# Attention by halves of the queries, in batches of four score units and four value units

## The reference

```
attn = einsum('bhnd,bhsd->bhns', q, k) * scale
attn = clip(attn, -11.0, 11.0)
attn = softmax(attn, axis=-1)
out  = einsum('bhns,bhsd->bhnd', attn, v)
x    = x + tanh(g_xattn) * (out @ Wo + bo)
```

## Time and profile before

| | |
|---|---|
| median of 3 runs (lowest to highest) | 1573.42 us (1571.2 to 1574.33) |
| profiled execution | 1573.17 us, span 1571.3 us |
| busy: TensorE / its weight loads | 1493.8 us (95%) / 868.4 us (55%) |
| busy: VectorE | 1323.4 us (84%) |
| busy: ScalarE | 701.4 us (45%) |
| busy: GpSimd | 132.6 us (8%) |
| mean granted TensorE clock | 0.992 |
| exps, 512 of them | 496.2 us |
| adds to prob_sum, 224 in the trace's group | 515.9 us |
| clips, 256 | 313.8 us |

### The profile page before, as it was taken

How to read it: one execution, slowest core, us unless ns; L and a number is a source line. 1 busy time by engine, 2 the same in 40 slices (tenths; PEclk the granted TensorE clock), 3 DMA queues, 4 the chain that set the end, 5 groups by cost and what they waited for, 6 DMA issues and landing times. The chain is left out here.

```text
span 1571.3 us, 22090 instructions
## 1 busy us (share of the span) xinstructions
PE 1493.8 (95%) x7888; PEld 868.4 (55%) x7896; DVE 1323.4 (84%) x1272; ACT 701.4 (45%) x778; POOL 132.6 (8%) x71
## 2 busy tenths in 40 slices
PE   3999999999998999999999999999999999998875
PEld 3788888888885344444444444444444444445553
DVE  7866667666746998999999999999999999997997
ACT  3442222222224555555555555555555555552221
POOL 2310000000001300000000000000000000005553
PEclk9999999999999999999999999999999999999998
DMA  5674565555587242253154044144234325105331
GB/s 191 243 255 169 172 190 161 189 158 168 165 241 221 80 122 69 68 135 98 50 121 121 27 121 121 45 103 121 66 82 126 77 65 135 41 28 134 128 113 53
DMA packets 121998, 195.30 MB, mean 124 GB/s; under 512 B 18368, under 2 KB 67520, under 8 KB 115808
## 3 DMA queue, kind: packets, MB, share of 16 engines
q1 hardware_dynamic: 119360, 190.49, 41.8%
q10 hardware_dynamic: 2592, 4.20, 0.7%
HBM read 114.70 MB, written 79.95 MB: 124 GB/s over the span
## 5 line engine op out<-in xcount | busy, mean ns | idle before, releaser
L932 ACT ACTIVATE prob<-score_ps 128x1024 f32<-128x1024 f32 x512 | 496.2, 1021 | 379.7 <-PE score_ps L861 379.5
L1016 DVE TENSOR_TENSOR prob_sum<-prob_sum,prob 128x2048 f32<-128x2048 f32 x224 | 515.9, 2303 | 0.5
L874 PE MATMUL value_ps<-prob,v_st 128*64 128x512 f32 x2048 | 497.4, 606 | 10.5 <-DVE prob L1022 10.1
L861 PE MATMUL score_ps<-q_st,k_st 64*128 64x512 f32 x3072 | 425.7, 409 | 2.5 <-PEq L102 2.1
L861 PEld LDWEIGHTS score_ps<-q_st,k_st 64*128 64x128 f32 x3072 | 268.7, 184 | 256.2 <-ACT prob L932 187.8
L1022 DVE TENSOR_SCALAR prob<-prob 128x2048 f32<-128x2048 f32 x256 | 313.8, 1226 | 68.1 <-ACT prob L932 64.2
L874 PEld LDWEIGHTS value_ps<-prob,v_st 128*64 128x64 f32 x2048 | 124.4, 136 | 250.5 <-issue 202.3
L645 DVE TENSOR_TENSOR k_cos<-k_raw,rope 128x1024 f32<-128x1024 f32 x32 | 39.2, 1225 | 99.9 <-ACT k_raw L546 99.9
L1305 POOL TENSOR_TENSOR o_lo<-o_in,o_hi 128x1024 fp32r<-128x1024 f32 x16 | 39.0, 2438 | 879.5 <-POOLq L115 872.6
L551 ACT ACTIVATE v_out<-proj_ps 128x1024 f32<-128x1024 f32 x31 | 32.0, 1031 | 136.6 <-PE proj_ps L228 136.6
L546 ACT ACTIVATE k_raw<-proj_ps 128x1024 f32<-128x1024 f32 x31 | 31.9, 1029 | 105.2 <-PE proj_ps L228 104.0
(11 more groups left out here) (118 smaller groups left out, 1294.1 us busy)
## 6 DMA issues: line engine op xcount, KB each, us to landing
k_st<-k_scr SPq DMA_DIRECT2D x128, 256.0 KB, 6.2
k_scr<-k_hi SPq DMA_DIRECT2D x64, 256.0 KB, 2.7
v_scr<-v_out SPq DMA_DIRECT2D x32, 512.0 KB, 3.5
k_scr<-k_lo SPq DMA_DIRECT2D x64, 256.0 KB, 3.9
q_st<-q_scr SPq DMA_DIRECT2D x16, 1024.0 KB, 10.3
v_st<-v_scr SPq DMA_DIRECT2D x16, 1024.0 KB, 13.2
q_scr<-q_hi SPq DMA_DIRECT2D x32, 256.0 KB, 3.6
q_scr<-q_lo SPq DMA_DIRECT2D x32, 256.0 KB, 3.7
```

Source lines behind the costliest of these rows:

```text
L861: last = pe.matmul(score_ps[:, half, a, :], k_st[slot][rows, k_part, s * P:(s + 1) * P], q_st[slot][rows, q_part, cols], start=(t == 0), s ...
L874: last = pe.matmul(value_ps[rows, cols], v_st[slot][:, s, rows], prob[:, s % PSLOT, a, cols], start=(s == 0), stop=(s == STEPS - 1))
L932: act.activation(prob[:, s % PSLOT, :, cols], score_ps[:, half, :, :], ACT.Exp, scale=SCALE).then_inc(exped, 1)
L1016: dve.tensor_tensor(total, total, prob[:, s % PSLOT, :, :], ALU.add).then_inc(added, 1)
```

## The change

Attention goes by halves of the queries. A unit is one key tile against 512 queries; a pair has 32 units, the first 16 for the first half. They are taken in 8 batches of four. TensorE does the scores of four units, then the values of the four units of the batch before. The scores have three slots of two banks, the values one bank, which is copied out after each half; the sums are taken for each half with 32 columns a matmul, in one bank, for both halves of `prob_sum`'s columns and both heads, and VectorE joins the two parts with a small add. The clip covers a whole batch (128 x 4096), the adds of the same batch follow it directly. `prob` holds two batches and has its former size. The chain of the reciprocals, the normalisation and the output store run once for each half of a pair, and the load two pairs ahead moves behind the first half's chain. All of `quantise_rhs` now stands in pair 0, three operations a batch.

```diff
-    PSLOT = 4
+    BATCH_UNITS = 4
+    UNITS = 2 * STEPS
+    BATCHES = UNITS // BATCH_UNITS
+    HALF_BATCHES = BATCHES // 2
+    BANKS = 3
+    ADDS = 2 * HALF_BATCHES - 1
-    prob = sb("prob", [P, PSLOT, 2, NQ])
-    prob_sum = sb("prob_sum", [P, 2, 2, NQ])
+    prob = sb("prob", [P, 2, BATCH_UNITS, 2 * CH])
+    prob_sum = sb("prob_sum", [P, 2, 2, 2, CH])
-    score_ps = ps("score_ps", [P, 2, 2, NQ // 2])
-    value_ps = ps("value_ps", [P, NQ])
-    sum_ps = ps("sum_ps", [P, NQ])
+    score_ps = ps("score_ps", [P, BANKS, 2, CH])
+    value_ps = ps("value_ps", [P, CH])
+    sum_ps = ps("sum_ps", [P, CH])
...
-    WO_STEPS = (3, 9, 11, 13)
+    WO_BATCHES = (1, 3, 4, 5)
...
+        def after(n, where, before, loading=None):
+            ends.store_sums(sp, n, 0)
+            ends.load_sums(sp, n, 0)
+            if before is not None:
+                ends.store_output(sp, n - 1, 1, *before)
+            ends.store_reciprocals(sp, n, 0)
+            ends.load_reciprocals(sp, n, 0)
+            if loading is not None:
+                load(n + 2, *loading)
+            ends.store_sums(sp, n, 1)
+            ends.load_sums(sp, n, 1)
+            ends.store_output(sp, n, 0, *where)
+            ends.store_reciprocals(sp, n, 1)
+            ends.load_reciprocals(sp, n, 1)
...
+        def scores(n, slot, b):
+            if b == 0:
                 pe.wait_ge(kqv_in[slot], KQV * (n // 2 + 1))
+            for u in range(b * BATCH_UNITS, (b + 1) * BATCH_UNITS):
+                half, s = divmod(u, STEPS)
+                cols = slice(half * CH, (half + 1) * CH)
+                if u >= BANKS:
+                    pe.wait_ge(exped, UNITS * n + u - BANKS + 1)
+                elif not first(n):
+                    pe.wait_ge(exped, UNITS * n - (UNITS - 1 - u) % BANKS)
...
+        def values(n, slot, b):
+            pe.wait_ge(clipped, BATCHES * n + b + 1)
+            if b % HALF_BATCHES == 0 and not (first(n) and b == 0):
+                pe.wait_ge(late.o_copied, 2 * n + b // HALF_BATCHES)
+            for i in range(BATCH_UNITS):
+                s = (b * BATCH_UNITS + i) % STEPS
                 for a in range(2):
                     rows = slice(a * DHEAD, (a + 1) * DHEAD)
+                    last = pe.matmul(value_ps[rows, :], v_st[slot][:, s, rows], prob[:, b % 2, i, a * CH:(a + 1) * CH],
                                      start=(s == 0), stop=(s == STEPS - 1))
...
+        def sums(n, half):
...
+            for j in range(2):
                 for a in range(2):
+                    row = (2 * j + a) * SUM_ROWS
+                    last = pe.matmul(sum_ps[row:row + SUM_ROWS, :], ones[:, 0:SUM_ROWS], prob_sum[:, half, j, a, :],
+                                     start=True, stop=True)
...
         def pair(n, slot):
+            for b in range(BATCHES):
+                scores(n, slot, b)
+                if b >= 1:
+                    values(n, slot, b - 1)
+                elif not first(n):
+                    values(n - 1, 1 - slot, BATCHES - 1)
+                if b == 1 and not first(n):
+                    sums(n - 1, 1)
+                if b == HALF_BATCHES + 1:
+                    sums(n, 0)
...
+        def exps(n, b):
+            for u in range(b * BATCH_UNITS, (b + 1) * BATCH_UNITS):
+                act.wait_ge(scored, UNITS * n + u + 1)
+                if u % BATCH_UNITS == 0 and not (first(n) and b < 2):
+                    act.wait_ge(valued, BATCHES * n + b - 1)
+                    act.wait_ge(added, ADDS * (2 * n + (b - 2) // HALF_BATCHES) + 2 * ((b - 2) % HALF_BATCHES) + 1)
...
         def pair(n, slot):
+            for b in range(BATCHES):
+                if b == 1 and not first(n):
+                    copy_values(n - 1, 1)
+                if b == HALF_BATCHES + 1:
+                    copy_values(n, 0)
+                if b == 2 and not first(n):
+                    copy_sums(n - 1, 1)
+                if b == HALF_BATCHES + 2:
+                    copy_sums(n, 0)
...
+                exps(n, b)
...
+        def clip(n, b):
+            tile = prob[:, b % 2, :, :]
+            dve.wait_ge(exped, UNITS * n + (b + 1) * BATCH_UNITS)
+            dve.tensor_scalar(tile, tile, CLIP_LOW, CLIP_HIGH, ALU.max, ALU.min).then_inc(clipped, 1)
+
+        def add_probs(n, b):
+            half, part = divmod(b, HALF_BATCHES)
+            total = prob_sum[:, half, :, :, :].rearrange("p j a c -> p j (a c)")
+            halves = [prob[:, b % 2, j:j + 2, :] for j in (0, 2)]
+            before = ADDS * (2 * n + half) + 2 * part - 1
+            dve.wait_ge(clipped, BATCHES * n + b + 1)
+            if part == 0:
...
+                dve.tensor_tensor(total, halves[0], halves[1], ALU.add).then_inc(added, 1)
+                return
+            for j in range(2):
+                dve.wait_ge(added, before + j)
+                dve.tensor_tensor(total, total, halves[j], ALU.add).then_inc(added, 1)
...
         def pair(n, slot):
+            for b in range(BATCHES):
+                clip(n, b)
+                add_probs(n, b)
+                if b == 7 and not (isinstance(n, int) and n == ALLPAIRS - 1):
+                    ends.reciprocals(dve, n, 0)
+                if b == 1 and not first(n):
+                    ends.normalise(dve, n - 1, 0)
+                if b == 3 and not first(n):
+                    ends.reciprocals(dve, n - 1, 1)
+                if b == 5 and not first(n):
+                    ends.normalise(dve, n - 1, 1)
+                if first(n):
+                    for k in range(3):
+                        quantise_rhs(3 * b + k)
```

More of the change, by code:

```diff
@@ L172, in load_reciprocals @@
+    def load_reciprocals(self, sp, n, half):
         late = self.late
-        sp.wait_ge(late.rec_stored, 16 * (n + 1))
+        sp.wait_ge(late.rec_stored[half], 16 * (n + 1))
         for a in range(2):
[L176 to L181, removed]
@@ L830, in _ @@
         for n in range(2):
[L831 to L833 removed]
+            after(n, (0, n), (0, n - 1) if n else None, (n, 0, n + 2))
         with sp.Fori(1, ALLPAIRS // 2 - 1) as i:
@@ L836, in _ @@
                 n = 2 * i + slot
[L837 to L841, removed]
+                here, last, ahead = [(sp.snap((n + d) // PAIRS), sp.snap((n + d) % PAIRS)) for d in (0, -1, 2)]
+                after(n, here, last, (slot,) + ahead)
+        n = ALLPAIRS - 2
+        after(n, (BATCH - 1, PAIRS - 2), (BATCH - 1, PAIRS - 3))
+        for half in range(2):
+            sp.wait_ge(late.o_stored[half], 16 * PAIRS)
         for t in range(2):
@@ L860, in scores @@
                         rows = slice(a * DHEAD, (a + 1) * DHEAD)
-                        last = pe.matmul(score_ps[:, half, a, :], k_st[slot][rows, k_part, s * P:(s + 1) * P],
+                        last = pe.matmul(score_ps[:, u % BANKS, a, :], k_st[slot][rows, k_part, s * P:(s + 1) * P],
                                          q_st[slot][rows, q_part, cols], start=(t == 0), stop=(t == len(TERMS) - 1))
                 last.then_inc(scored, 1)
[L865 to L871, removed]
+        def values(n, slot, b):
[4 more added lines that the diff above has]
+                s = (b * BATCH_UNITS + i) % STEPS
@@ L872, in values @@
                 for a in range(2):
                     rows = slice(a * DHEAD, (a + 1) * DHEAD)
-                    last = pe.matmul(value_ps[rows, cols], v_st[slot][:, s, rows], prob[:, s % PSLOT, a, cols],
+                    last = pe.matmul(value_ps[rows, :], v_st[slot][:, s, rows], prob[:, b % 2, i, a * CH:(a + 1) * CH],
                                      start=(s == 0), stop=(s == STEPS - 1))
             last.then_inc(valued, 1)
[L878 to L882, removed]
+        def sums(n, half):
+            pe.wait_ge(added, ADDS * (2 * n + half + 1))
+            if not (first(n) and half == 0):
+                pe.wait_ge(late.sum_copied, 2 * n + half)
+            if first(n, 2) and not first(n) and half == 0:
@@ L889, in sums, with turn_rhs @@
             last.then_inc(summed, 1)
-        def pair(n, slot):
[L892 to L914, removed]
+        def turn_rhs(part):
+            pe.wait_ge(late.sum_copied, 2)
+            if part == 0:
+                pe.wait_ge(rhs_step, KT + 2 + 3 * KT)
+            else:
+                pe.wait_ge(rhs_copied, 1)
+            for k in range(KT // 2):
+                for t in range(KT):
+                    rows = slice((part * KT // 2 + k) * P, (part * KT // 2 + k + 1) * P)
+                    last = pe.transpose(rhs_ps[:, k, t, :], rhs_int[:, t, rows], ident_bf[:, :])
+            last.then_inc(rhs_turned, 1)
@@ L921, in _ @@
     def _(act):
[L922 to L932, removed]
@@ L1286, in turn @@
             if isinstance(t, int) and t == 3:
-                ends.reciprocals(dve, LAST)
+                for half in range(2):
+                    ends.reciprocals(dve, LAST, half)
             ending = isinstance(t, int) and t == TILES + 1
```

202 lines of the change are left out of this document (96 added, 106 removed).

## The result

The changed kernel takes **1547.69 us** (median of four runs, 1546.72 to 1549.71) against 1572.34 before in the same series: ratio 0.984, 95% interval 0.9821 to 0.9859. It is faster by 1.6%, within the range, and 13.7 us slower than forecast: of the 38.6 us that I expected, about 25 came.

What follows compares the result with a forecast made beforehand. TensorE was taken to set the pace, VectorE right behind it. Gains of 13 x 2.55 in the loop, 3 in pairs 0 and 1 and 2.4 in the last make 38.6 us: 1573.2 - 38.6, so 1534 us, range 1522 to 1560.

Steps and rivals of the forecast that it cites:

- TensorE's sum: TensorE per pair of heads: eight batches of 6.565 us plus two groups of sums at 1.0, 54.5 us against 57.06.
- The 0.34 of the changes of shape: TensorE, each step: going from one tile shape to the other and back costs about 0.34 us, which the change can remove.
- the one on the three score slots: Fourth score unit of a batch: slot released at 2.16 us, wanted at 2.20, so cost 0; bounds 0 and 0.15 a batch.
- the score slots are short: Rival: waiting for a score slot costs 0.1 to 0.15 us a batch, giving 1547 to 1553 us; chance 0.13.
- 52.7 forecast: VectorE's work per pair of heads: 52.7 us, 1.8 below TensorE.
- the 96% that I named as a sign: Sign that the prediction is right: VectorE 96% busy.
- VectorE becomes the bound: Rival: VectorE's large operations cost more than reckoned and it sets the pace, 1540 to 1560 us; chance 0.15.
- where I had 2.2: Clip of a batch on VectorE: may be 2.2 us late before TensorE's values of that batch need it.
- The transfers: SyncE's reciprocal chain: loads issued 8.8 us after the pair's start, store landed at 26.8, sums back at 29, wanted at 32.8.
- the slower rival: Rival at VectorE's reciprocal in the fourth batch: sums come back late, slower once 8.2 us later than reckoned; chance 0.10.
- The ends: Pairs outside the loop: pair 0 stays at 64.4 us, pair 1 becomes 56.8, together 3 less; last pair 62.0, 2.4 less.

Runs made afterwards that it cites:

- reordered kernel: The changed kernel with ScalarE's wait for the scores put after those for values and adds, before a batch's first exp: 1535.92 us, ratio 0.9769.

## Why the prediction was right, and where it was off

**TensorE's sum.** The terms held: values 3.58 (forecast 3.58), sums 1.00 (1.0), scores with a free slot 2.97 (2.985), a pair 54.61 (54.5) once the slots are free. The 0.34 of the changes of shape came back as 0.35 when one pair of them was added. That four 32-column tiles run together, which no row of before showed, is shown by the 1.00 against 1.81 of the run with 64 columns; the Trainium skill (TensorEngine Tiling (Array Packing), Tiling Modes) says so as well.

**The step that was mis-sized** is the one on the three score slots: "cost 0, by 0.04 us only". I took the exp's start from one step of the kernel before, 1.09 after the scores. It came at 1.17, ended at 2.20 instead of 2.11, and the release at 2.25 missed the 2.20 at which TensorE wants the slot. The loss is the lateness of 0.06 plus the 0.11 of a first interval, up to 0.17 a batch and 0.12 in the mean: 12.5 us over the loop, nearly all of the 13.7 that were missing. What is left of the loop's shortfall fits that I set a sum (54.5) against a measured pair (57.06): the same sum for the kernel before, 16 x 3.45 + 1.73, gives 56.93, so 0.13 a pair was counted as gain that was none. It is the rival "the score slots are short" with the size given to it (0.1 to 0.15; 1547 to 1553). What I did not see is that the number depends on the place, and the trace of the kernel before shows it. Outside the loop the first exp starts 1.00 after the scores (490.81 in the earlier trace rows):

```profile
489.81 1.66 PE L861 MATMUL score_ps<-q_st,k_st 64*128 64x512 f32 x12 [2.11 <-PEq L102]
```

In the loop it starts 1.09 or 1.10 after them in most steps, 1.00 to 1.02 in two (one is the step behind the sums), and 1.16 to 1.17 in the first three steps of a pair, the exp at 907.49 among them. So the 1.17 of the changed kernel was there to be read before the change, and with it the release comes at 2.25 and not at 2.16. A margin of 0.04 should have cost that step its certainty, and the rival should have had the larger chance. Why the same waits cost between nothing and 0.17 from place to place was not tested.

**VectorE** took 52.6 a pair (52.7 forecast), by the run with the added operation. It shows as busy for 674 of the 722.5 us from 618 to 1340.5, 93% and not the 96% that I named as a sign. The rival "VectorE becomes the bound" did not happen, and is 2.0 us away in the reordered kernel. The clip in two halves shows that the clip is covered. How far varies over a half: the clip at 915.88 ends 2.4 us before its values start (920.54), the next one, at 923.14, only 1.8 before them (927.18), where I had 2.2 without the lateness of that batch. The hand-over in one piece made TensorE wait for nothing in the loop, so the advice of the Trainium skill (Perfetto Trace Analysis, Optimizing Scalar/DVE Operations) to break up instructions where they cause bubbles found no bubbles to remove.

**The transfers** came nearly as reckoned. The first scores of a pair and SyncE's issues after:

```profile
889.55 3.25 PE L885 MATMUL score_ps<-q_st,k_st 64*128 64x512 f32 x24
...
898.80 3.91 SPq L94 DMA_DIRECT2D k_st<-k_scr  x8
...
904.96 8.33 SPq L160 DMA_DIRECT2D sum_scr<-sum_row  x1
917.13 0.40 SPq L165 DMA_DIRECT2D sum_sq<-sum_scr  x1
```

The loads are issued 9.25 after the pair's start (forecast 8.8, though the parts that I gave, 5.9 + 1.9 + 1.25, add up to 9.05), the store has landed by 27.6 (26.8), and VectorE takes up the sums at 922.83, 33.3 after it (32.8) and without idle time. The small loads land in 1.9 us although their pieces are half as large. The issue of that load ends at 917.53, so the sums are there at about 919.4, and 3.4 us were in hand against the slower rival (3.8 forecast).

**The ends.** Pair 0 runs from the first scores at 490.05 to 552.9 (559.56 less a batch and the 0.1 before the copy), 62.8 us instead of the 64.4 that I left unchanged. Pair 1 takes 58.6 (618.15 - 559.56), not 56.8: VectorE comes out of pair 0 behind, and the values of its first batch wait 1.36 for the clip, which is most of the difference:

```profile
561.63 2.29 DVE L1047 TENSOR_SCALAR prob<-prob 128x4096 f32<-128x4096 f32 x1
...
563.97 3.65 PE L897 MATMUL value_ps<-prob,v_st 128*64 128x512 f32 x16 [1.36 <-DVE prob L1047]
```

So I put 1.6 too much on one and 1.8 too little on the other: that the two together came out as forecast was luck. Attention ends at 1395.64, 55.1 after the last pair's copy; with 6.7 ahead of it the last pair takes 61.8 (forecast 62.0). By terms the gain is 13 x 1.49 = 19.4 in the loop (33.2 forecast), 3.1 in pairs 0 and 1 (3), and 2.6 in the last (2.4): 25.1 of the 25.3 us between the spans of 1571.3 and 1546.0.

## What to carry to other kernels

Where matmuls of two tile shapes alternate, count the interval at each change against the plain interval; if the sum matters, put several units of one shape together, as far as the slots of PSUM and the engine behind them allow. A slot that is to come free just in time is a risk: a release 0.06 us too late cost 0.17 here, its lateness and a long first interval besides. Before a margin of some hundredths of a microsecond is relied on, the delay that it rests on should be read at many steps and not at one. Put the wait that comes last behind all others on its engine, above all in a loop, where waits compare with computed values.

## What I had not expected

Two waits that had long been satisfied cost about 0.17 us when they stood between the scores and the exp in the loop (exp 1.17 after the scores, 1.00 with them moved ahead or outside the loop). In the kernel before they cost 0.15 at the step shown and bought nothing when moved. Moving one line gave 12 us, and the kernel with them moved, 1535.92 us at ratio 0.9769, beats the kernel before and the changed kernel.
